# Second cross attention: which units TensorE turns, and which engine keeps them and the queries

## What is computed

```
xn = layernorm(x) * gamma + beta
q = (xn @ w_q).reshape(B, 56, 16, 64);  k, v = split(context @ w_kv)      # context: (32, 1500, 128)
attn = softmax(einsum('bqhd,bkhd->bhqk', q * SCALE, k))
out = einsum('bhqk,bkhd->bqhd', attn, v).reshape(B, 56, 1024) @ w_out + b_out
x = layernorm(x + out * tanh(gate))
```

## Time and profile before

| | |
|---|---|
| median of 3 runs | 1882.11 us (1882.07 to 1885.69) |
| the profiled execution's own time | 1884.88 us |
| its span | 1883.0 us |
| TensorE busy | 1667.1 us (89%) |
| VectorE busy | 1549.9 us (82%) |
| ScalarE busy | 1275.3 us (68%) |
| GpSimd busy | 925.5 us (49%) |
| DMA queue of SP | 632204 packets, 281.10 MB, 64.2% of 16 engines' span |
| mean granted TensorE clock | 0.96 of full speed |

### The profile page before, as it was taken

The page is one execution under the profiler, slowest core; times in us unless marked ns, Lnnn a source line. Parts: engine busy times, 40 slices in busy tenths (PEclk is TensorE's granted clock), DMA queues, the critical chain, the costliest instruction groups (busy, mean ns, idle before and its releaser), DMA issues. The chain is left out here.

```text
span 1883.0 us, 34675 instructions
## 1 busy us (share of the span) xinstructions
PE 1667.1 (89%) x10425; PEld 1009.4 (54%) x10425; DVE 1549.9 (82%) x2885; ACT 1275.3 (68%) x2106; POOL 925.5 (49%) x723
## 2 busy tenths in 40 slices
PE   4987996889957899999999999999999999994997
PEld 2654665777733344554554554454455455454886
DVE  2765785877758999999999999999999999975887
ACT  2442332877735887887888788788788888864554
POOL 3640111363335766565665656656567465421333
PEclk9997998799978999999999999999999999997998
DMA  5203884311100898988899898898888889973231
GB/s 190 95 0 127 306 332 173 85 42 45 45 34 17 180 197 174 199 182 179 190 183 190 183 190 187 178 195 182 179 199 179 188 183 185 182 135 122 47 79 29
DMA packets 632266, 281.85 MB, mean 150 GB/s; under 512 B 601852, under 2 KB 606236, under 8 KB 631452
## 3 DMA queue, kind: packets, MB, share of 16 engines
q1 hardware_dynamic: 632204, 281.10, 64.2%
HBM read 129.02 MB, written 1.05 MB: 69 GB/s over the span
## 5 line engine op out<-in xcount | busy, mean ns | idle before, releaser
L2237 DVE SCALAR_TENSOR_TENSOR xa_h<-xa_psum,xa_rinv,xa_h 128x500 f16<-128x500 f32 x672 | 452.8, 730 | 1.0 <-ACT xa_h L2445 0.7
L2445 ACT ACTIVATE xa_h<-xa_psum,xa_rinv 128x1000 f16<-128x1000 f32 x448 | 371.5, 883 | 51.8 <-DVE xa_rinv L2228 51.5
L2429 ACT ACTIVATE xa_psum<-xa_psum,xa_bias,unscale_s 128x1500 f32<-128x1500 f32 x224 | 353.2, 1577 | 7.4
L2073 PE MATMUL xa_psum<-xa_c_hi,xa_q_hi 128*128 128x500 f16 x672 | 257.4, 383 | 54.5 <-DVE xa_h L2237 50.1
L2217 DVE TENSOR_REDUCE xa_psum<-xa_psum 128x1 f32<-128x1000 f32 x224 | 269.3, 1202 | 14.2 <-PE xa_psum L2075 13.4
L2098 PE MATMUL xa_psum<-xa_prT,xa_n_hi 128*128 128x512 f16 (+1 forms) x768 | 270.8, 353 | 3.6 <-issue 1.6
L2100 PE MATMUL xa_psum<-xa_prT,xa_n_lo 128*128 128x512 f16 (+1 forms) x768 | 270.6, 352 | 0.0
L2099 PE MATMUL xa_psum<-xa_prT,xa_n_hi 128*128 128x512 f16 (+1 forms) x768 | 270.6, 352 | 0.0
L2074 PE MATMUL xa_psum<-xa_c_lo,xa_q_hi 128*128 128x500 f16 x672 | 252.7, 376 | 0.0
L2075 PE MATMUL xa_psum<-xa_c_hi,xa_q_lo 128*128 128x500 f16 x672 | 252.4, 376 | 0.0
L1939 POOL TENSOR_SCALAR xa_ctxT<-xa_ctxT,scales 128x1500 f32<-128x1500 f32 x31 | 126.3, 4073 | 166.4 <-DMA xa_ctxT<-in_ctxT 166.4
(11 more groups left out here) (328 smaller groups left out, 3630.4 us busy)
## 6 DMA issues: line engine op xcount, KB each, us to landing
ctxN<-in_ctxP SPq DMA_DIRECT2D x16, 1536.0 KB, 9.5
xa_ctxP<-in_ctxP SPq DMA_DIRECT2D x32, 768.0 KB, 4.3
ctxT<-in_ctxT SPq DMA_DIRECT2D x16, 1500.0 KB, 6.4
xa_ctxT<-in_ctxT SPq DMA_DIRECT2D x32, 750.0 KB, 4.7
moe_spread<-weight_rows SPq DMA_DIRECT2D x16, 1024.0 KB, 8.4
xa_prT<-xa_h SPq DMA_TRANSPOSE x192, 5.5
up<-in_F_up SPq DMA_DIRECT2D x1, 2048.0 KB, 7.7
down<-in_F_down SPq DMA_DIRECT2D x1, 2048.0 KB, 11.8
```

What stands on the lines that cost most here:

```text
L2073: nc.tensor.matmul(out, qh, c_hi[:, b, a:z], start=True, stop=False)
L2237: nc.vector.scalar_tensor_tensor(low, psum[:, bank + a:bank + z, 0:W], rinv[:, s % 2, :], high, ALU.mult, ALU.subtract).then_inc(h2_ready, 1)
L2429: nc.scalar.activation(psum[:, bank:bank + 3, 0:W], psum[:, bank:bank + 3, 0:W], ACT.Exp, bias=bias[:, s % 2, :], scale=k.unscale_s[:, :], ...
L2445: nc.scalar.activation(h[:, H_SLOT[s], 0, a * W:z * W].rearrange("p (a c) -> p a c", c=W), psum[:, bank + a:bank + z, 0:W], ACT.Identity, ...
```

## The change

Unit 4 is no longer turned by TensorE: its probabilities go by a DMA transpose, which SP issues in slot 4, ahead of that slot's load. Unit 11 stays with TensorE, but its thirds are copied by ACT, at the head of its step, ahead of that slot's exponentials, and not by DVE. The queries of a pair are kept in one ACT instruction of 448 columns in place of two of 224. Waits on TensorE that protect bank 7 are rewritten to suit; the waits of the first pair on the end of the state phase move from DVE to ACT.

```diff
-    TURNED = (GA, UPS + GA)
-    ROUNDS = {GA: (GA + 2, GA + 6, GA + 7), UPS + GA: (NU - 1, NU, NU + 1)}
+    TURNED = (UPS + GA,)
+    ROUNDS = {UPS + GA: (NU - 1, NU, NU + 1)}
...
# TensorE, turn
-                if u == TURNED[0] and r == 0:
-                    pe.wait_ge(turn_kept[TURNED[1]], last(i, NR, NR))
-                    if not end:
-                        pe.wait_ge(q_kept, q_count(i + 1, NB - 1))
-                if u == TURNED[0] and r == 1 and not first:
-                    pe.wait_ge(t.r_ready, this(i - 1))
-                if u == TURNED[1] and r == 0:
-                    pe.wait_ge(turn_kept[TURNED[0]], this(i, NR, NR))
-                    if not first:
-                        pe.wait_ge(t.logits_kept, this(i - 1))
+                if r == 0 and first:
+                    pe.wait_ge(q_kept, q_count(i + 1, NB - 1))
+                elif r == 0:
+                    pe.wait_ge(t.logits_kept, this(i - 1))
# TensorE, step
-                        pe.wait_ge(turn_kept[TURNED[1]], last(i, NR, NR))
+                        pe.wait_ge(turn_kept[TURNED[0]], last(i, NR, NR))
...
                     if s == min(OUTPUT):
-                        pe.wait_ge(turn_kept[TURNED[0]], this(i, 1, NR))
+                        if end:
+                            pe.wait_ge(turn_kept[TURNED[0]], last(i, NR, NR))
+                        else:
+                            pe.wait_ge(q_kept, q_count(i + 1, NB - 1))
...
-                    pe.wait_ge(turn_kept[TURNED[0]], this(i, NR, NR))
+                    pe.wait_ge(t.r_ready, this(i - 1))
# VectorE: keep_turned and its calls (step, epilogue) removed, and in between(2)
-                    dve.wait_ge(tok_stored, CHUNKS)
-                    dve.wait_ge(xT_ready, CHUNKS)
# ScalarE
+            def keep_turned(i, u, r):
+                act.wait_ge(turn_ready[u], this(i, r + 1, NR))
+                nc.scalar.activation(
+                    prT[:, P_SLOT[u], :, :].rearrange("p (x k) c -> p k x c", x=2)[:, r * KT // NR:(r + 1) * KT // NR, :, :],
+                    turn_bank, ACT.Copy).then_inc(turn_kept[u], 1)
...
-                for b in range(2):
-                    done = nc.scalar.activation(
-                        q_full[:, b, :, c * HB:(c + 1) * HB].rearrange("p s h -> p h s"),
-                        psum[:, bank, 0:HB * 2 * S].rearrange("p (h b s) -> p h b s", h=HB, b=2)[:, :, b, :],
-                        ACT.Copy, scale=1.0 / Q_UNIT)
+                done = nc.scalar.activation(
+                    q_full[:, :, :, c * HB:(c + 1) * HB].rearrange("p b s h -> p h b s"),
+                    psum[:, bank, 0:HB * 2 * S].rearrange("p (h b s) -> p h b s", h=HB, b=2), ACT.Copy, scale=1.0 / Q_UNIT)
...
             def step(i, s, first=False, end=False):
+                at = turn_at(*unit(i, s - 1))
+                if at and (s >= UPS or not first):
+                    keep_turned(*at)
                 exponentials(i, s)
...
# ScalarE, between(1)
+                    act.wait_ge(tok_stored, CHUNKS)
# ScalarE, epilogue
+                for r in range(NR):
+                    keep_turned(PAIRS - 1, TURNED[0], r)
```

More of the change, by code:

```diff
@@ L2209, in _ @@
             open_sems(dve, NL * NU, h2_ready)
-            open_sems(dve, NR, *turn_kept.values())
             t.open_vector(dve)
@@ L2238, in low_part @@
                                                    ALU.mult, ALU.subtract).then_inc(h2_ready, 1)
[L2240 to L2245, removed]
             def residual(i):
@@ L2257, in step @@
                     inverse(*unit(i, s - 1))
-                at = turn_at(*unit(i, s - 1))
-                if at and (s >= UPS or not first):
-                    keep_turned(*at)
                 if s == RESIDUAL and not first:
@@ L2378, in epilogue @@
                 inverse(i, NU - 1)
-                keep_turned(i, TURNED[1], 0)
                 low_part(i, NU - 1)
-                keep_turned(i, TURNED[1], 1)
-                keep_turned(i, TURNED[1], 2)
                 residual(i)
@@ L2394, in _ @@
             open_sems(act, NG, on_kept)
+            open_sems(act, NR, *turn_kept.values())
             t.open_scalar(act)
+            def keep_turned(i, u, r):
[3 more added lines that the diff above has]
+                    turn_bank, ACT.Copy).then_inc(turn_kept[u], 1)
             def evacuate(i, g):
```

## The result

The changed kernel takes 1897.9 us (median of 4 runs, 1894.5 to 1900.07) against 1883.2 for the kernel before in the same comparison: a ratio of 1.0075, 95% interval 1.0055 to 1.0094. The forecast was 1890.8, slower, with a range from 1874 to 1902: a loss of 8.7 us, where the medians show 14.7. The profiled execution took 1898.64 us (before 1884.88), 13.8 more, with a span of 1896.7.

The account below looks back on a forecast made before the run. No busy share named the bound; by slots it was mostly a DVE-ACT ring, TensorE in slots 7 to 9, ACT in slot 3. Fifteen pairs at +0.66 us (+9.9), -1.8 and +0.6 make +8.7: 1890.8 us, range 1874 to 1902.

Parts of the forecast that it names:

- The wait: DVE's residual waits 2.1 us a pair for POOL's xg, as the ctxP load goes out 6.1 us later.
- 4 us later in the slot: Sign: SP's slot-4 load should start 4 us later in the slot, behind a transpose that waited for TensorE.
- The load lands sooner: Rival, chance 0.16: ctxP lands under 4.5 us after issue, the residual's wait falls to 1.2 us, time 1877.3 us.
- Slots 10 and 11: Without unit 4's copies at the head of slots 11 and 12, the ring gains 1.24 us a pair; slots 4.4 us.
- Slots 6 and 7: Unit 4's copy at the head of slot 7 goes but frees nothing, as TensorE bounds behind it: 0.
- ACT's copies: Unit 11's three copies on ACT take 1.03 us each, slot 4.95 against 5.01: counted 0, bounds -4 to +9 us.
- The estimate of 1.15: Alternative price of one ACT copy from the Trainium skill, 1.15 us; the sum would be 5 us higher.
- the rival of the dear copy: Rival, chance 0.10: ACT's copy costs 0.2 us more on each of three slots, +9, 1900 us; TensorE starts queries late.
- Queries: One ACT instruction of 448 columns, about 0.62 us, takes 0.2 us a pair off slot 3 alone.
- Transposes: Unit 5's transpose lands late, ACT waits some 0.6 us for unit 8's buffer, hidden; DMA share 0.93.
- The first pair: The first pair has no residual and loses three copies of 0.6 us: -1.8 us.
- the ring: Plain slot's loop, 4.39 us: DVE's maximum, ACT's bias and exponentials, DVE's reciprocal, next maximum; a copy inside costs 0.62 us.

Follow-up runs that it names:

- experiment 5: The changed kernel with unit 11's three copies on DVE again instead of ACT: 1895.14 us, 1.0059; with the ctxP load also ahead of the transpose, 1865.26 us, 0.9896.
- experiment 6: The changed kernel with the queries in two ACT instructions of 224 columns again: 1900.66 us, 1.008 of the kernel before.
- experiment 1: The changed kernel with SP's slot-4 ctxP load issued ahead of unit 4's transpose: 1866.88 us, 0.9902 of the kernel before.
- experiment 7: The changed kernel with no unit turned by TensorE, all 14 by DMA transpose, both ctxP loads ahead of their slot's transpose: 1842.4 us, 0.9782 of the kernel before.
- experiment 3: The kernel before the change with only one ctxP load made late, in slot 5 behind unit 5's transpose: 1948.24 us, 1.0324.
- experiment 8: The kernel of experiment 7 with both ctxP loads put back behind the transposes: 1905.03 us, 1.0111; then with POOL making xg first, 1853.15 us, 0.9829.

## Why the prediction was right, and where it was off

*The wait.* Forecast 2.1 us for the residual, measured 30.3 / 15 = 2.02. Each link was as told: SP's transpose waited for the last values of slot 6, the load followed 4.00 us after the transpose's start (1041.43 to 1045.43; forecast 4.0), and POOL began 1050.79 - 1045.43 = 5.36 us after it (5.07 in the median of 14 pairs; forecast 5.1, from slot 1's load). From POOL's start to the end of xg it took 9.39 us (forecast 9.38). Counted from unit 5's maximum the load went out 6.05 us later than before, as the working has it (6.1); the "4 us later in the slot" among the signs doesn't agree with that working, and 4 us is the step from the transpose's start to the load.

*The load lands sooner.* This rival fell. Loads of ctxP land in 4.1, 4.6 and 5.2 us (least, median, most, from 700 to 1500 us), where the earlier trace rows have 4.1, 4.3 and 4.7. Taken apart, slot 4's, with a transpose issued 0.59 us behind it, land in 4.7 to 5.2 us (median 4.9), and slot 11's, with 3.5 us or more to the next transpose, in 4.1 to 4.5 (median 4.3): about 0.6 us between them. The rule of the Trainium skill on which the rival rested (DMA: Bandwidth & Descriptors, Queues, rings and completion order) is only that an engine takes up a ring's descriptors in order; that a later transpose would therefore not delay the load was my own step, and these loads speak against it. No run separates whether the delay comes from the order of the descriptors or from the traffic.

*Slots 10 and 11.* Forecast 1.24 us less for the two, measured 10.02 - 8.82 = 1.20. Behind the last residual, where the clock fell to 0.66 over 5 us, slot 10 took 5.32 us; the forecast had no term for that.

*Slots 6 and 7.* Forecast 0 for the copy that went. Units 6 to 8: 5.02 + 4.63 = 9.65 us before, 4.40 + 5.24 = 9.64 after. All of it went into the wait for TensorE, 0.78 us at unit 8's maximum. So the forecast of 0 is right, but its sign that slots 7 and 8 stay at 4.6 and 5.0 is not: the slot from unit 7's maximum took 5.24.

*ACT's copies.* Counted at 0, and here a little was missing. One copy takes 1024 ns (forecast 1.03). The estimate of 1.15 was too high: the row of the Trainium skill that it used (ScalarE: Activation LUTs, Rules for kernel authors) is for an activation whose bias is a pointer operand, and this copy has none. The first two slots with a copy on ACT are 4.90 and 4.97 us (forecast 4.95). They lie one slot later than with DVE's copies, from unit 0's maximum on; the slot from unit 13's maximum, for which the signs had 5.0, fell to 4.46. ACT's third copy, at the head of slot 2, is what TensorE's first projection waits for, and the scores behind it come late:

```profile
1023.30 0.22 PE L2057 MATMUL xa_psum<-xa_x_hi,kq_hi 128*128 x1 [0.82 <-ACT xa_prT L2382]
```

That slot, from unit 2's maximum to unit 3's, takes 5.23 us, and the four slots together 19.56 instead of 19.41: +0.15 us a pair. The prediction named TensorE's late start only in the rival of the dear copy. But ACT is not the reason for most of the 0.15: with DVE copying in the same kernel the four take 19.5 too (experiment 5), so at most 0.06 of it is ACT's, and no run places the rest.

*Queries.* Forecast 0.2 us a pair less, measured nothing: slot 3, where ACT bounds (between the maxima of units 4 and 5), takes 4.70 us for 4.74, and with two instructions again 4.69 (experiment 6), so the 0.04 is not the merge's. The mistake was to take an instruction's price from a row of 512 columns at 678 ns; this one takes 918 ns for 448. Its output is scattered; that this is the reason is likely and not tested.

*Transposes.* Unit 8's high part waited up to 0.85 us for its buffer, in 8 of 14 pairs (forecast 0.6), hidden as expected; the DMA share rose to 0.92 (forecast 0.93).

*The sum.* Forecast +8.7 us, and 13.7 between the two spans. Read by DVE's maxima, the 14 pairs in the middle take 956.3 us for 945.4: +11.0, 0.78 a pair where the forecast had 0.66. The slot of the residual gives +1.85 of that, slots 10 and 11 -1.20, and the four slots with copies +0.14. The residual's slot grew by less than its wait, since without a wait it is 5.41 us in experiment 1, 0.14 shorter than the 5.55 before; the forecast had no term for that either, and no run places it. The first pair gives -2.5 (forecast -1.8), the last +3.2 (0.7), as its wait was the longest and the clock fell behind it, the end behind the last maximum +1.1 (0.6), and +0.8 lies before the stage. So the mechanism and the size of the main term were right, and the sum was low by the queries (3 us), the four slots with copies (2 us) and the last pair (2.5 us); the residual's shorter slot goes the other way (2 us), and that it does is luck.

## What to carry to other kernels

Read the queue behind every wait that an edit adds. Here a transpose that waits for TensorE held a load, the load held GpSimd, and one small instruction behind it in GpSimd's list (0.46 us) held DVE, and with it ACT and TensorE. A load goes ahead of a transpose that must wait, and work that is ready and due goes ahead of a wait for a DMA; each of the two edits turned a loss of 0.75% into a gain of 1%.

Judge a resource by who waits for it and not by its busy share: the DMA engines read 0.88 to 0.92 and looked nearly full, yet the kernel of experiment 7, with two more transposes a pair than before, is 2.2% faster.

## What the runs showed that I had not expected

- TensorE's granted clock fell behind the residual's waits (0.64 to 0.68 over 5 us in the windows shown): behind 13 of 15 in experiment 3 (3.3 to 3.8 us), 14 of 15 in experiment 8 (1.7 to 3.0), and 1 of 15 in the changed kernel (1.8 to 2.4; in its variants of experiments 5 and 6, with the load still late, behind 3 and 2). It stayed 1.00 behind waits of 3.25 and 3.30 us and fell behind one of 1.73, so the length of the wait doesn't decide it, and what does stays open. A wait in the ring can so cost more than its length: with the two slots behind, 60.5 us for 52.6 of waiting in experiment 3, and 51 for 36 in experiment 8.
- The busy share of the DMA engines passes 1 (1.04 over 130 us), so a share of 0.9 is no measure of the room that is left.
- One ACT instruction of 448 scattered f32 columns takes 918 ns, more than the evacuation's 512 columns (678 ns), and as much as two of 224 that overlap.
- The ctxP loads landed later where a transpose was issued within 1 us behind them: medians of 4.6 to 5.0 us over the kernels here, against 4.2 to 4.5 with nothing behind them for 2.3 us or more.
